# Score matmuls of four heads on four banks, with down-projections and P.V moved to shared banks

## What is computed

```python
x = x + _layernorm(_L0_attn_ref(_layernorm(x), ...))
x = x + _layernorm(_L0_ffn_ref(_layernorm(x), ...))
x = x + _layernorm(_L1_attn_ref(_layernorm(x), ...))
x = x + _layernorm(_L1_ffn_ref(_layernorm(x), ...))

def _L1_ffn_ref(x, ...):
    h = x + attention(rmsnorm(x, ln1_w), ...)
    return h + moe(rmsnorm(h, ln2_w), ...)

def attention(x, ...):              # 16 heads of 16, causal, S = 512
    kv_d, q_d = x @ kv_d_w, x @ q_d_w             # latents of 64
    k = concat([kv_d @ k_u_w, rope(x @ rope_k_w)])
    q = concat([q_d @ q_u_w, rope(q_d @ rope_q_w)])
    v = kv_d @ v_u_w
    scores = where(causal, q @ k.T * 16 ** -0.5, min)
    return (softmax(scores) @ v) @ o_w

def moe(x, ...):                    # one shared expert, 7 routed, top 2
    w = top2(sigmoid(x @ router_w + router_b)), normed
    for e: out += w[e] * ((silu(x @ wg[e]) * (x @ wu[e]) / 8) @ wd[e])
```

## Time and profile before

| | us |
|---|---|
| median of 3 runs | 2077.3 (2073.2 to 2081.3) |
| the profiled execution | 2074.5 |
| its span | 2072.7 |
| PE busy | 1760.1 (85%) |
| DVE busy | 1392.3 (67%) |
| ACT busy | 1174.9 (57%) |
| POOL busy | 613.5 (30%) |

### The profile page before, as it was taken

One profiled execution on the slowest core, in us unless ns is written; L12 is line 12 of the kernel. 1 busy time (PEld: TensorE's weight loads), 2 busy tenths in 40 slices (PEclk: granted clock), 3 DMA queues, 4 the chain that ended last, 5 costly groups with the idle time before them and its releaser, 6 DMA issues. The chain is left out here.

```text
span 2072.7 us, 26422 instructions
## 1 busy us (share of the span) xinstructions
PE 1760.1 (85%) x7634; PEld 1209.2 (58%) x7634; DVE 1392.3 (67%) x3597; ACT 1174.9 (57%) x2846; POOL 613.5 (30%) x1916
## 2 busy tenths in 40 slices
PE   5878878788975888988898889788699999999987
PEld 2545445355654666866786678566356555555554
DVE  6565665222336999999999999997333554555546
ACT  3242442111025999999999999997155453553530
POOL 3423324000013455454544554543200102002000
PEclk9677896899987899998999899999899999999999
DMA  6000000000010000000000000000000000000000
GB/s 251 1 0 0 0 0 1 0 0 0 0 61 1 1 1 1 1 1 1 1 1 1 1 1 1 1 1 1 0 1 1 1 1 1 1 11 1 11 1 21
DMA packets 6851, 19.76 MB, mean 10 GB/s; under 512 B 960, under 2 KB 3904, under 8 KB 5440
## 3 DMA queue, kind: packets, MB, share of 16 engines
q1 hardware_dynamic: 6720, 18.23, 2.3%
HBM read 16.13 MB, written 2.10 MB: 9 GB/s over the span
## 5 line engine op out<-in xcount | busy, mean ns | idle before, releaser
L1282 ACT ACTIVATE mem_arena<-mem_arena,r_shift 128x256 f32<-128x256 f32 x864 | 385.2, 511 | 23.8 <-POOL r_shift L1221 23.8
L1052 DVE BATCH_NORM_STATS2 r_moments<-mem_arena 128x6 f32<-128x512 f32 x576 | 380.1, 690 | 10.4 <-ACT mem_arena L1282 7.5
L1361 PE MATMUL r_bank<-G,r_wT 128*128 128x256 f32 x1024 | 233.3, 387 | 3.7 <-ACT mem_arena L1282 2.7
L1361 PEld LDWEIGHTS r_bank<-G,r_wT 128*128 128x128 f32 x1024 | 195.7, 194 | 35.3 <-issue 8.6
L1587 DVE CUSTOM_DVE_ANT_0 e_seen<-e_banks,mask_q 128x512 f32<-128x512 f32 (+3 forms) x256 | 112.7, 487 | 101.0 <-PE e_banks L2094 100.4
L1377 PE MATMUL r_bank<-ident,mem_arena 128*128 128x128 f32 x576 | 110.4, 324 | 71.5 <-DVE mem_arena L1068 71.1
L1908 ACT ACTIVATE mem_arena<-e_banks 128x512 f32<-128x512 f32 x160 | 91.4, 593 | 135.1 <-PE e_banks L2111 135.0
L1029 DVE MAX8 r_top<-r_bank 128x8 f32<-128x256 f32 x384 | 144.9, 404 | 18.0 <-PE r_bank L1361 17.8
L1897 ACT ACTIVATE e_rows_p<-e_seen,e_NM 128x512 f32<-128x512 f32 (+3 forms) x256 | 125.6, 554 | 51.0 <-DVE e_NM L1587 50.8
L1371 PE MATMUL r_bank<-G,ident 128*128 128x256 f32 x384 | 142.3, 458 | 11.8 <-ACT r_wT L1308 11.5
L1377 PEld LDWEIGHTS r_bank<-ident,mem_arena 128*128 128x128 f32 x576 | 81.1, 166 | 113.6 <-DVE mem_arena L1068 104.0
(11 more groups left out here) (292 smaller groups left out, 3450.5 us busy)
## 6 DMA issues: line engine op xcount, KB each, us to landing
w<-in_w SPq DMA_DIRECT2D x3, 1024.0 KB, 14.5
out_x<-X SPq DMA_DIRECT2D x4, 512.0 KB, 2.9
X<-in_x SPq DMA_DIRECT2D x1, 1536.0 KB, 11.9
w_in<-in_w_in SPq DMA_DIRECT2D x1, 1156.0 KB, 6.7
mem_arena<-in_wq SPq DMA_DIRECT2D x1, 1024.0 KB, 16.7
mem_arena<-in_wo SPq DMA_DIRECT2D x1, 1024.0 KB, 21.3
gate<-in_gate SPq DMA_DIRECT2D x1, 1024.0 KB, 4.7
up<-in_up SPq DMA_DIRECT2D x1, 1024.0 KB, 6.8
```

The costliest lines, as they stand in the source:

```text
L1052: last = dve.bn_stats(moments[:, a.lane, 2 * p:2 * p + 2, :].rearrange("p two c -> p (two c)"), u[a.lane][:, 2 * p:2 * p + 2, :].rearrange ...
L1282: last = act.activation(u[a.lane][:, h, :], u[a.lane][:, h, :] if k else scores[:, h, :], ACT.Relu, bias=shift[:, a.lane, h:h + 1])
L1361: last = pe.matmul(scores[:, h, :], lhs, (G1 if a.first else G2)[:, h, i, :], start=i == 0, stop=i == 1)
```

## The change

- The eight banks are dealt anew: four for scores (0 to 3, one for each head), two rotating (4, 5), one for gate (6) and one for up (7).
- `look` takes a part instead of items and computes it for all four heads, with the heads innermost: three calls a group instead of six. It waits until all four items of the part before have been taken.
- The halves of a down-projection go to the banks of gate and up (`down_bank`); gate and up of expert e wait for the `combine` halves of expert e-2, and down halves of expert e for `gated` and `hide` of expert e+1.
- P.V goes to a rotating bank, as a twelfth user in each round, between turn 9 and turn 0.
- In `middle`, the transposes of x go to banks 2 and 3, values to 4 and 5, the router's logits to 5, the rope parts to 7 and 6 in turn with 0 and 1.
- The orders are rewritten for this: on DVE `hide(e0)` comes ahead of takes 4 and 5, `gated(e1)` ahead of takes 8 to 11, `choose` and `out_rows` to the end of their group; on ACT copies and exponentials alternate more finely; on PE see the last part of the diff.

```diff
--- before.py
+++ after.py
@@ -1520,14 +1524,22 @@
 
             return a * NG + g
 
+        def t_bank(a, g, r):
+
+            return TURN + t_use[a, g, r] % 2
+
+        def part_banks(n):
+            return (UP, GATE) if n % 2 == 0 else (0, 1)
+
         def gate_bank(b, e):
+
             return GATE if b + 1 < B or e % 2 == 0 else 0
 
         def up_bank(b, e):
             return UP if b + 1 < B or e % 2 == 0 else 1
 
         def down_bank(b, half):
-            return DOWN if b + 1 < B or half == 0 else VALUES
+            return (GATE, UP)[half] if b + 1 < B else 2 + half
 
         def heads_of(g):
...
@@ -1465,7 +1469,7 @@
 
         banks = ctx.enter_context(nc.psum_tensor("e_banks", [P, 8, 512], F32))
         bank = [banks[:, i, :] for i in range(8)]
-        LOOK, TURN, VALUES, GATE, UP, DOWN = 0, 2, 4, 5, 6, 7
+        LOOK, TURN, GATE, UP = 0, 4, 6, 7
         stats = sb("e_stats", [P, TPB, 6])
         ostats = sb("e_ostats", [P, TPB, 6])
...
@@ -1585,7 +1597,7 @@
                     for i, c0 in LOOKS[n // 4]:
                         width = (i + 1) * P
                         last = dve.tensor_tensor_reduce(out=seen[:, j, c0:c0 + width],
-                                                        in0=bank[LOOK + n % 2][:, c0:c0 + width],
+                                                        in0=bank[LOOK + j][:, c0:c0 + width],
                                                         in1=T["mask_q"][:, S - width:], scale=-1.0, scalar=-MASKED,
...
@@ -1715,27 +1727,25 @@
                     take(a, g, 2, 3)
                     if work:
                         gated(b, e0)
+                        hide(b, e0)
                     take(a, g, 4, 5)
-                    if work:
-                        hide(b, e0)
-                        if g:
-                            combine(b, e0 - 1, 0)
+                    if work and g:
+                        combine(b, e0 - 1, 0)
                     take(a, g, 6, 7)
                     if work and g:
                         combine(b, e0 - 1, 1)
                     if g:
                         divide(a, g - 1)
+                    if work:
+                        gated(b, e1)
+                    take(a, g, 8, 9, 10, 11)
+                    if work:
+                        hide(b, e1)
+                        combine(b, e0, 0)
                     if work and g == 0:
                         choose(b)
                     if work and b and g == 2:
                         out_rows(b - 1)
-                    take(a, g, 8, 9)
-                    if work:
-                        gated(b, e1)
-                    take(a, g, 10, 11)
-                    if work:
-                        hide(b, e1)
-                        combine(b, e0, 0)
                     if g == 1 and a + 1 < B:
                         row_stats(a + 1)
...
@@ -1940,28 +1950,35 @@
             def overlap(b):
                 a, work = b + 1, b >= 0
                 for g in range(NG):
+                    weigh(a, g, 0)
                     if g:
                         keep(a, g - 1, 8)
-                    weigh(a, g, 0, 1)
+                    weigh(a, g, 1)
                     if g:
                         keep(a, g - 1, 9)
-                    weigh(a, g, 2, 3)
+                    weigh(a, g, 2)
                     if work:
                         open_gate(b, 2 * g)
+                    weigh(a, g, 3)
                     if g:
                         attention_out(a, g - 1)
-                    keep(a, g, 0, 1)
-                    weigh(a, g, 4, 5)
-                    keep(a, g, 2)
-                    weigh(a, g, 6, 7)
-                    keep(a, g, 3)
-                    keep(a, g, 4, 5)
-                    weigh(a, g, 8, 9)
+                    keep(a, g, 0)
+                    weigh(a, g, 4)
+                    keep(a, g, 1)
+                    weigh(a, g, 5)
+                    keep(a, g, 2, 3)
+                    weigh(a, g, 6)
                     if work:
                         open_gate(b, 2 * g + 1)
+                    weigh(a, g, 7)
+                    keep(a, g, 4)
+                    weigh(a, g, 8)
+                    keep(a, g, 5)
+                    weigh(a, g, 9)
                     keep(a, g, 6)
-                    weigh(a, g, 10, 11)
+                    weigh(a, g, 10)
                     keep(a, g, 7)
+                    weigh(a, g, 11)
                 keep(a, NG - 1, 8, 9)
                 attention_out(a, NG - 1)
...
@@ -1990,7 +2007,7 @@
 
             def columns(b):
                 pe.wait_ge(R["xr"], b + 1)
-                to_columns(5).then_inc(R["xT_in_psum"], 1)
+                to_columns(2).then_inc(R["xT_in_psum"], 1)
 
             def latents(b):
...
@@ -2080,20 +2097,20 @@
                     keys_or_queries(b + 1, 4)
                     keys_or_queries(b + 1, 5)
 
-            def look(a, g, *ns):
-
-                for n in ns:
-                    L = seq(a, g) * NL + n
-                    if g == 0 and n == 0:
-                        pe.wait_ge(R["kq"], (a + 1) * NP)
-                    elif L >= 2:
-                        pe.wait_ge(R["take"], L - 1)
-                    j = n % 4
-                    hp = slice(SLOT * j, SLOT * (j + 1))
-                    for i, c0 in LOOKS[n // 4]:
-                        last = pe.matmul(bank[LOOK + n % 2][:, c0:c0 + (i + 1) * P], QT[hp, g, i * P:(i + 1) * P],
+            def look(a, g, part):
+
+                L = seq(a, g) * NL + 4 * part
+                if g == 0 and part == 0:
+                    pe.wait_ge(R["kq"], (a + 1) * NP)
+                else:
+                    pe.wait_ge(R["take"], L)
+                for i, c0 in LOOKS[part]:
+                    for j in range(4):
+                        hp = slice(SLOT * j, SLOT * (j + 1))
+                        last = pe.matmul(bank[LOOK + j][:, c0:c0 + (i + 1) * P], QT[hp, g, i * P:(i + 1) * P],
                                          KT[hp, g // 2, 0:(i + 1) * P], start=True, stop=True)
-                    last.then_inc(R["look"], 1)
+                        if (i, c0) == LOOKS[part][-1]:
+                            last.then_inc(R["look"], 1)
 
...
+                        last = pe.transpose(o[:, j * P:(j + 1) * P], rows_p[:, j, P_AT[i] + kb * P:P_AT[i] + (kb + 1) * P], ident[:])
                     last.then_inc(R["tr"], 1)
 
             def weigh(a, g):
 
                 pe.wait_ge(R["copied"], (seq(a, g) + 1) * NT)
-                if seq(a, g):
-                    pe.wait_ge(R["ot"], seq(a, g))
-                if g == 0:
-                    pe.wait_ge(R["v"], at(a, 2, 2))
+                t_free(t_use[a, g, "values"])
+                o = bank[t_bank(a, g, "values")]
                 for kb in range(TPB):
                     for j, head in enumerate(heads_of(g)):
-                        last = pe.matmul(bank[VALUES][SLOT * j:SLOT * (j + 1), kb * P:], V[:, kb, head, :], PT[kb][:, j, :],
+                        last = pe.matmul(o[SLOT * j:SLOT * (j + 1), kb * P:], V[:, kb, head, :], PT[kb][:, j, :],
                                          start=kb == 0, stop=kb == TPB - 1)
                 last.then_inc(R["pv_done"], 1)
 
             def values_to_rows(a, g):
                 pe.wait_ge(R["ot"], seq(a, g) + 1)
-                t_free(t_use[a, g, NT])
+                t_free(t_use[a, g, "rows"])
+                o = bank[t_bank(a, g, "rows")]
                 for i in range(TPB):
-                    last = pe.transpose(bank[TURN + o_bank[a, g]][:, i * P:(i + 1) * P], OT[:, i * P:(i + 1) * P], ident[:])
+                    last = pe.transpose(o[:, i * P:(i + 1) * P], OT[:, i * P:(i + 1) * P], ident[:])
                 last.then_inc(R["o_rows"], 1)
 
             def gate_half(b, e, k):
-                if k == 0 and b + 1 < B and e:
-                    pe.wait_ge(R["gated"], at(b, NEXP, e))
-                elif k == 0 and b + 1 == B and e >= 2:
+                if k == 0 and b + 1 < B and e >= 2:
+                    pe.wait_ge(R["acc"], at(b, NEXP * 2, 2 * (e - 2) + 1))
+                elif k == 0 and b + 1 < B and e:
+                    pe.wait_ge(R["gated"], at(b, NEXP, 1))
+                elif k == 0 and e >= 2:
                     pe.wait_ge(R["gated"], at(b, NEXP, e - 1))
                 last = pe.matmul(bank[gate_bank(b, e)], gate[:, e, k, :], hT[:, k, :], start=k == 0, stop=k == KD - 1)
                 if k:
                     last.then_inc(R["gate_done"], 1)
 
             def up_half(b, e, k):
-                if k == 0 and e == 0:
-                    pe.wait_ge(R["logits"], b + 1)
-                elif k == 0 and b + 1 < B:
-                    pe.wait_ge(R["hidden"], at(b, NEXP, e))
+                if k == 0 and b + 1 < B and e >= 2:
+                    pe.wait_ge(R["acc"], at(b, NEXP * 2, 2 * (e - 2) + 2))
+                elif k == 0 and b + 1 < B and e:
+                    pe.wait_ge(R["hidden"], at(b, NEXP, 1))
```

(43 more changed lines are left out.)

35 lines of the change are left out of this document (13 added, 22 removed).

## The result

The changed kernel takes 2012.3 us (2010.8 to 2015.8) against 2075.4 for the kernel before, a ratio of 0.969 with a 95% interval of 0.967 to 0.972: 63 us less, where 53 were forecast. The forecast was 2024 us, its first case 2013 to 2036: 2012.3 lies just under that, in the case "better than 2013" that had 0.03, and inside the range of 2009 to 2050. The profiled execution takes 2013.5 us, its span is 2011.6.

What follows compares the result with a forecast made beforehand. TensorE was taken as the bound in the four `overlap` stages; savings of 14.3, 17.0, 15.8 and 10 made 57 us, 53 after an allowance, so 2077.3 became 2024 us, range 2009 to 2050.

Steps and rivals of the forecast that it cites:

- first case: Whole kernel: the forecast's own outcome, a time of 2013 to 2036 us, chance 0.62.
- better than 2013: Whole kernel: a time under 2013 us, since low clock starts could vanish (4.7 us each, twice), chance 0.03.
- The merging: Score matmuls in `look`: three calls replace six, saving call time and shape changes, 3.4 of 24.4 us a group.
- rival A: Score matmuls: four strips not served together, pairs follow pairs, 2.1 us a full group, 29 in all, 2053 us, chance 0.10.
- The walk: Regular group followed step by step on PE, DVE and ACT: 21.0 us, with no slack at two points.
- turn 4: PE's turn 4 in each group: ACT's chain ends at 17.4 us, PE arrives at 17.36, 0.0 of room.
- gate(e1): Gate matmul of the group's expert e1: waits for `combine`(e0-1, 0), 12.3 against 13.1 us, 0.8 of room.
- The 0.1 of room at P.V: P.V in a rotating bank: ACT's last copy done at 5.46 us, PE there at 5.55.
- the allowance of 0.3 us: Some 15 groups: 0.3 us each taken off the saving for two points without slack, 57 to 53 us.
- B: Groups at P.V and turn 4: ACT and DVE stall PE 1.5 to 2 us, 24 more, 2048 us, chance 0.17.
- C: Gate and up banks: waits for `combine` delay both by turns, slower, say 1.4 us at each of four waits, 2088, chance 0.04.
- D: Shorter stages: three or four more groups at low clock, 4.7 us each, nothing comes of it, 2062 to 2072, chance 0.04.

Runs made afterwards that it cites:

- before_dve_end: The kernel before with only VectorE's order changed, `choose` and `out_rows` at the end of their groups: 2078.7 us, 1.003 of the kernel before.
- the one with eight products: The changed kernel with eight more unused 128x256 products on VectorE ahead of take 4 in all 16 groups: 2031.2 us, 0.978 of the kernel before.

## Why the prediction was right, and where it was short

**The merging** was sized at 3.4 us a regular group and measured at 3.3 (six calls); the kernel before took 24.4 in its regular group, 3.4 more than the changed one. The bound for pairs behind pairs, 2.1 us, was not touched: rival A is out.
The prediction set the Trainium skill's 3.07 times (TensorE: Matmul & The Clock Gate, Measured speedup vs the span model) beside this; here four heads of 512 columns take 1.07 us where one after the other they would take 3.4 (an estimate: four times the gate half's 0.86), 3.2 times as long, and the measured 1.07 stands.

**The walk** gave 21.0 for the regular group, 15.8, 22.75 and 27.8 for the first, second and last of batch 0, 0.9 for `out_rows`; the trace has 21.0, 15.9, 22.7, 27.75 and 0.9. Stage by stage, as forecast and as measured: 10 and 12.3, 14.3 and 14.4, 17.0 and 20.0, 15.8 and 19.4 (each to the last group's end on PE, where the earlier trace rows and the windows above round). Two of its critical points were tried, turn 4 and gate(e1): taking the room away there (ScalarE +0.5, VectorE +1.3 and +2.6) gives what it says to 0.3 us in a group. The 0.1 of room at P.V was not tried.

**The step that was mis-sized** is the allowance of 0.3 us for each of 15 groups, 4 us, for a walk without slack at two points: no group slipped. Room of 0.0 was enough. The last exponential that turn 4 needs ended at 1668.39 in the changed kernel, the turn began at 1668.51 behind an up half, and PE had no idle time before it:

```profile
1667.49 0.90 ACT L1907 ACTIVATE e_rows_p<-e_seen,e_NM 128x384 f32<-128x384 f32 x2
...
1668.51 1.04 PE L2129 MATMUL e_banks<-ident,e_rows_p 128*128 128x128 f32 x8
```

From look 0 these are 17.3 and 17.4 us, where the walk had 17.4 and 17.36. That the step times of the earlier trace rows already held the semaphores would explain it; it was not tested. Without the allowance the sum is 57. Batch 2 was also taken 0.7 too low: the 1.3 us by which its stage is shorter in the earlier trace rows are 0.6 from the first look to the last transposition of the stage, and the rest lies behind it.

**The other ten** are TensorE's clock, which I had left as it was. The first groups of batches 1 and 2 ran at a granted clock of 0.79 before, and again in the second profile of that kernel; in the changed kernel at 0.90, in both its profiles (above). They cost 1.7 us there over batch 0's first group, where the earlier trace rows had 4.7: 3.0 twice. The first stage gave 2.3 more than counted and the middle stage ahead of it 1.9; in both, the lower clock lasted a shorter time. That makes 10, and 57, 10 and batch 2's 0.7 are the 67.6, with the last batch's end 0.4 longer. Of these ten, 4 are not shown to be the change's: `before_dve_end`, which is the kernel before up to the first stage with experts, has the same 1.9 and 2.2 of them; and its batch 2 begins at full clock, so the 3.0 of that batch can be doubted too. And a low stretch stood inside the 7.4 counted for the third group of batch 1 too: after the wait of 1.42 us that `out_rows` made, an up half took 1.87 us to the next operation:

```profile
1822.83 1.14 PE L2094 MATMUL e_banks<-e_KT,e_QT 32*128 32x256 f32 x4 [1.42 <-DVE e_NM L1587]
1823.90 2.08 PE L2151 MATMUL e_banks<-e_hT,up 128*128 128x512 f32 x2
1825.77 1.06 PE L2111 MATMUL e_banks<-ident,e_rows_p 128*128 128x128 f32 x4
```

That window was at 0.94, and the changed kernel has 1.00 there.

With `choose` moved, both first groups ran at full clock, in a block whose first groups differ only in where `choose` stands on VectorE:

```profile
1723.10:1739.00 15.90, 14.98 (x84) 8.11 (x84) 12.63 (x48) 11.62 (x24) 0.00 (x0) 1.00 0.01 2
```

So the low stretch at a stage's start doesn't belong to that group's work. Each of two kernels showed it twice at the same place, but code that is the same up to the place also showed it for different times (`before` and `before_dve_end`, the changed kernel and the one with eight products). What decides it, the kernel or chance, was not settled here. PE's wait of 2.1 us for the last query rows stands just ahead of each stage, of those that begin at full clock too, so it alone doesn't decide.

**The rivals.** B (ACT and DVE become the bound) did not happen, but the two loads show how near it was: ACT had nothing to spare at turn 4, DVE 1.0 us at gate(e1). Beside it the prediction had the rule of the Trainium skill (TensorEngine Tiling (Array Packing), PSUM Bottleneck) by which the reading of PSUM may set the pace after such a gain; here it did so nowhere in the regular group, where PE is busy 21.0 of 21.0 us. C (gate and up banks) shows as the 1.31 us in front of gate(e1) once DVE is 2.6 us later, and in the second groups as the 1.40 in front of up(e0), which the walk had as 1.75 of `choose`; it never came to the 4.5 us a group from which it would have decided. D (the low clock eats the gain) did not happen either: the first groups went from 0.79 to 0.90, and no group became low that was not. By D's own terms, 24 and four times 4.7, its upper end would have been 2067 and not 2072, and the chances for "below 2067" add up to 0.94, not 0.93.

**What the parts are worth,** inside the block: merging 40.3; the clock, as far as it can be told apart, about 10 (some of it in the 40.3, since the version with six calls had low starts of its own); the rest, 17 to 20, is `out_rows` no longer in front of a look (about 2.6 net in each of batches 1 and 2: 3.5 in the third group, which `before_dve_end` gives, less 0.9 in the fourth; the low stretch behind the wait is part of the 3.5), the waits on takes and `choose` in first groups, and the ends of the stages. Each was seen in its group; they were not undone one by one.

## What to carry to other kernels

Here score matmuls of 32 rows took 1.06 us for two heads and 1.07 for four, and two passes of a full 128-row matmul of the same columns 0.86: put as many row strips side by side as there are banks for them, and count the change of shape on both sides of a call (0.2 us here) as part of its price. Where a single engine is full, a step-by-step walk of all engines through one period, with start-to-start times from the trace, gives the new period and the waits with little or no room (21.0 us forecast and measured); look at those points for the next gain, and an allowance on top of such a walk was not needed here. Long work of another engine goes where that engine waits anyway: 6.8 us here for moving two pieces. And before a few microseconds are given to a change, the granted clock of the stretches must be compared: it moved the block by 4 us in code that was the same.

## What the runs showed of the hardware

Sixteen 32-row matmuls of 384 and 128 columns, issued head after head, overlap as if they were issued strip by strip (1.10 and 1.08 us). The lower clock came in the same place in two profiles of the same kernel, and in the version with the heads outermost (17.5 us for the first groups of batches 1 and 2); up to the first stage with experts it differed between `before` and `before_dve_end`, whose code is the same until there (29.3 and 21.1 us against 27.4 and 18.9). It cost up to 4.7 us a stage. The same code ahead of the block of experts took 1472 to 1485 us over the twelve profiles, while the block repeated within 0.1 us in the two profiles of each kernel.
